# Attention work of a pair moved earlier in the next pair's sums: projection at a pair's end, latents at the next pair's head, key products ahead of the choice

## The reference

```
W = weight * mask[None]                      # weight 16x5000x128, mask 5000x128
h = einsum('bg,egp->bep', x, W) + bias       # 64 x 16 tokens x 128
h = h + attention(layernorm(h))              # causal over the 16 tokens
h = h + ffn(layernorm(h))                    # 64 experts, two per token, and a shared one
```

## Time and profile before

| | us |
|---|---|
| median of 3 runs | 253.7 (252.67 to 255.78) |
| profiled execution | 254.11 |
| its span, first to last instruction | 252.4 |
| PE busy, of 2479 matmuls | 184.7 (73%) |
| DVE busy | 152.0 (60%) |
| POOL busy | 144.1 (57%) |
| ACT busy | 82.4 (33%) |
| mean granted TensorE clock | 0.891 |

### The profile page before, as it was taken

One profiled execution on the slowest core, in us unless ns is written; L12 is line 12 of the kernel. 1 busy time (PEld: TensorE's weight loads), 2 busy tenths in 40 slices (PEclk: granted clock), 3 DMA queues, 4 the chain that ended last, 5 costly groups with the idle time before them and its releaser, 6 DMA issues.

```text
span 252.4 us, 6075 instructions
## 1 busy us (share of the span) xinstructions
PE 184.7 (73%) x2479; PEld 153.9 (61%) x2479; DVE 152.0 (60%) x366; ACT 82.4 (33%) x245; POOL 144.1 (57%) x117
## 2 busy tenths in 40 slices
PE   0057877279989789695896699388976987999810
PEld 0057866169878678584785488257755766678410
DVE  0024382975696888979939928768796249011291
ACT  2004200023343333341331232538664444335500
POOL 3326479259979779999678783103114242074570
PEclk9999999977999999999599599657996599999965
DMA  7999999999999999999999999593011128213432
GB/s 237 256 342 418 361 421 334 403 417 417 417 419 422 417 419 416 426 417 413 396 226 220 227 194 145 153 265 145 4 42 52 55 70 243 87 42 96 139 96 53
DMA packets 32981, 65.11 MB, mean 258 GB/s; under 512 B 2874, under 2 KB 25367, under 8 KB 32375
## 3 DMA queue, kind: packets, MB, share of 16 engines
q1 hardware_dynamic: 31416, 59.47, 71.5%
q10 hardware_dynamic: 576, 3.26, 3.1%
q0 software_dynamic: 960, 1.97, 3.0%
HBM read 56.96 MB, written 7.73 MB: 256 GB/s over the span
## 4 chain that ended last, share of the span: by engine, by line
PE 39%; DVE 19%; DMA 16%; SPq 8%; ACT 7%; issue 4%; POOL 3%; POOLq 1%; DVEq 0%; ACTq 0%
DMA ring<-in_L_tok_weight_dram 15%; PE bank L833 13%; PE bank L1021 4%; SPq L360 4%; PE bank L991 4%; DVE bank L1233 3%; DVE prod L1227 3%; DVE ring L1206 3%; DVE prod L1251 2%; DVE bank L1259 2%; PE bank L1005 2%; SPq L366 2%; PE bank L971 2%; PE bank L876 2%; POOL ring L529 2%
## 5 line engine op out<-in xcount | busy, mean ns | idle before, releaser
L464 POOL TENSOR_TENSOR ring<-ring,mask 128x896 f32<-128x896 f32 (+1 forms) x48 | 91.6, 1933 | 19.0 <-DMA ring<-in_L_tok_weight_dram 19.0
L833 PE MATMUL bank<-ring,xT 128*64 128x128 f32 x1248 | 83.8, 294 | 9.9 <-DVE ring L1206 7.6
L833 PEld LDWEIGHTS bank<-ring,xT 128*64 128x64 f32 x1248 | 76.4, 149 | 14.6 <-DVE ring L1206 9.2
L1206 DVE TENSOR_TENSOR ring<-ring,bank 128x1024 f32<-128x1024 f32 (+1 forms) x45 | 45.7, 1049 | 35.5 <-DMA ring<-in_L_tok_weight_dram 35.5
L453 POOL TENSOR_TENSOR rstd<-mv,half 128x1 f32<-128x1 f32 (+1 forms) x24 | 14.2, 599 | 38.9 <-DVE mv L1214 23.4
L529 POOL DMA_INDIRECT ring<-expert_outputs,slot_index x16 | 16.0, 1002 | 16.9 <-DMA expert_outputs<-ring 8.0
L484 POOL DMA_INDIRECT expert_inputs<-xf,slot_index x14 | 14.3, 1021 | 9.9 <-DVE slot_index L1311 6.9
L814 PE MATMUL bank<-cst,w 64*128 64x64 f32 x39 | 5.3, 328 | 16.1 <-DMA w<-in_x_dram 15.4
L1021 PE MATMUL bank<-w2p,ring 64*64 64x128 f32 (+1 forms) x256 | 14.5, 291 | 3.4 <-ACT ring L705 2.1
L506 POOL TENSOR_TENSOR mask<-ring,mask 128x256 f32<-128x256 f32 x8 | 6.0, 756 | 16.3 <-ACT ring L699 16.3
L991 PE MATMUL bank<-w,ring 128*64 128x128 f32 (+1 forms) x256 | 14.9, 298 | 0.3 <-POOL mask L506 0.3
(11 more groups left out here) (151 smaller groups left out, 302.6 us busy)
## 6 DMA issues: line engine op xcount, KB each, us to landing
ring<-in_L_tok_weight_dram SPq DMA_DIRECT2D x48, 832.0 KB, 13.2
expert_inputs<-w ACTq DMA_DIRECT2D x3, 1024.0 KB, 9.9
ring<-expert_inputs SPq DMA_DIRECT2D x6, 512.0 KB, 5.4
expert_outputs<-ring SPq DMA_DIRECT2D x12, 256.0 KB, 2.3
mask<-in_L_tok_mask_dram SPq DMA_DIRECT2D x3, 832.0 KB, 16.1
w<-in_x_dram SPq DMA_DIRECT2D x1, 1250.0 KB, 13.6
w2p<-in_L_ffn_w_dram SPq DMA_DIRECT2D x1, 1024.0 KB, 18.9
xT<-masks_dram SPq DMA_DIRECT2D x1, 1024.0 KB, 7.9
```

The costliest lines, as they stand in the source:

```text
L464: pool.tensor_tensor(unit(j, q, SPLIT(q // 2), UC), unit(j, q, SPLIT(q // 2), UC), mask[:, (m + SPLIT(q // 2)) * D:(m + UC) * D], ALU.mult ...
L833: last = pe.matmul(bank[0][64 * par:64 * par + 64, 0:D], xT[:, (UC * t + c) * B:(UC * t + c + 1) * B], unit(j, 2 * t + par, c, c + 1), sta ...
L1206: dve.tensor_tensor(both(j, t, a, b), both(j, t, a, b), m.rearrange("p (u f) -> p u f", u=1).to_broadcast([P, 2, (b - a) * D]), ALU.mult). ...
```

## The change

- `project(c-1)` stands at the end of step c, and `turn_xn(c-1)` ahead of its last quarter, in every step from 1 on; so far this was so in step 7 alone, and the others had it at the head of step c+1. `norm_h` and `copy_xnT` move with it on ScalarE, to both sides of `probs`.
- `turn_qk(b)` stands at the head of the step between `turn_o` and `attend`, `qkv(b)` behind quarter 0, `values(b)` behind quarter 1, the gate behind quarter 2, `rank_tokens(d)` behind quarter 3.
- VectorE: `scores` is split; `multiply_keys(b)` and `stats_h(a)` come ahead of `choose(d)`, `sum_scores(b)` behind `place(d)`. Of its pieces one moves each from the third place to the second (`VECTOR_SHARE` 2, 1, 2, 1 to 2, 2, 1, 1).
- GpSimd: one piece, `root_qk`, one piece, `root_h2`, four pieces, in place of three pieces, `root_h2`, `root_qk`, three pieces.
- The order after the steps is as it was.

```
-POOL_SHARE = (3, 3)
-VECTOR_SHARE = (2, 1, 2, 1)
+POOL_SHARE = (1, 1, 4)
+VECTOR_SHARE = (2, 2, 1, 1)
...
                 mask_pieces(POOL_SHARE[0])
-                if d >= 0:
-                    root_h2(d)
                 if b >= 0:
                     root_qk(b)
                 mask_pieces(POOL_SHARE[1])
+                if d >= 0:
+                    root_h2(d)
+                mask_pieces(POOL_SHARE[2])
...
+                if b >= 0:
+                    square_qk(b)
+                    norm_qk(b)
                 if d >= 0:
                     copy_oT(d)
                 if b >= 0:
-                    copy_xnT(b)
-                    square_qk(b)
+                    turned_qk(b)
                 if d >= 0:
                     norm_xf(d)
                 if b >= 0:
-                    norm_qk(b)
+                    heads_k(b)
                 if d >= 0:
                     copy_xfT(d)
                 if b >= 0:
-                    copy_qkv(b)
-                if c == NCH - 1:
+                    heads_v(b)
+                if a >= 0:
                     norm_h(a)
-                    copy_xnT(a)
                 if b >= 0:
                     probs(b)
-                if 0 <= a < NCH - 2:
-                    norm_h(a)
+                if a >= 0:
+                    copy_xnT(a)
...
-                mask_pieces(VECTOR_SHARE[2])
+                if a >= 0:
+                    stats_h(a)
+                if b >= 0:
+                    multiply_keys(b)
                 if d >= 0:
                     choose(d)
-                if a >= 0:
-                    stats_h(a)
+                mask_pieces(VECTOR_SHARE[2])
                 if d >= 0:
                     place(d)
                 if b >= 0:
-                    scores(b)
+                    sum_scores(b)
                     less_max(b)
```

More of the change, by code:

```diff
@@ L606, in copy_xnT @@
                 act.copy(xnT[:], bank[3][:, 0:P]).then_inc(s_xnTs, 1)
-            def copy_qkv(j):
-                turned_qk(j)
-                heads_k(j)
-                heads_v(j)
             def turned_qk(j):
@@ L926, in _ @@
                     pe.wait_ge(s_qw, 16 * 6)
-                    pe.wait_ge(s_centred, 2)
-                project_b, attend_d = b >= 0, d >= 0
+                project_a, qkv_b, attend_d = c >= 1, b >= 0, d >= 0
                 if attend_d:
                     turn_o(d)
-                if project_b:
-                    turn_xn(b)
+                if qkv_b:
+                    turn_qk(b)
                 if attend_d:
                     attend(d)
-                if project_b:
-                    project(b)
-                for n in range(4):
-                    sum_genes(c, n)
+                sum_genes(c, 0)
+                if qkv_b:
+                    qkv(b)
+                sum_genes(c, 1)
                 if attend_d:
                     turn_xf(d)
-                if project_b:
-                    turn_qk(b)
-                sum_genes(c, 4)
+                if qkv_b:
+                    values(b)
+                sum_genes(c, 2)
                 if attend_d:
                     gate(d)
-                if project_b:
-                    qkv(b)
+                sum_genes(c, 3)
                 if attend_d:
                     rank_tokens(d)
-                sum_genes(c, 5)
-                if project_b:
-                    values(b)
-                for n in range(6, 12):
+                for n in range(4, 12):
                     sum_genes(c, n)
-                    if c == NCH - 1 and n == 10:
+                    if project_a and n == 10:
                         turn_xn(c - 1)
-                if c == NCH - 1:
+                if c == 1:
+                    pe.wait_ge(s_centred, 2)
+                if project_a:
                     project(c - 1)
@@ L1217, in over_keys, with multiply_keys @@
                 return q.rearrange("p (a h) d -> p a h d", a=1).to_broadcast([P, n, NH, q.shape[2]])
-            def scores(j):
+            def multiply_keys(j):
                 n, f = 2 * j + 2, NH * DK
@@ L1228, in scores, with sum_scores @@
                 dve.tensor_tensor(pr[:, :, :, DH:DK], keys[:, :, :, DH:DK], over_keys(turned, n), ALU.mult).then_inc(s_prod, 1)
+            def sum_scores(j):
+                n, f = 2 * j + 2, NH * DK
                 dve.wait_ge(s_prod, j + 1)
@@ L1236, in scores @@
                 then(dve.memset(raw(j)[0:64].rearrange("p (h s) -> p h s", h=NH)[:, :, n - 1:n], NEG))
+            def scores(j):
+                multiply_keys(j)
+                sum_scores(j)
             def less_max(j):
```

## The result

The changed kernel takes 265.72 us (median of 4 runs, 264.71 to 275.11) against 253.19 for the kernel before beside it (250.98 to 255.78): ratio 1.0512 [1.0413, 1.0612], **slower by 5%**. I had said 255.4, with a range to 261. The profiled execution spans 262.9 us at a mean clock of 0.867, where before had 252.4 and 0.891. Medians are of all executions, while a ratio and its interval leave out those, like the one of 275.11, in which a kernel ran slower as a whole.

The account below looks back on a forecast made before the run. DMA was taken to pace the early steps, a ring of waits among engines those from 4 on. 254.1 less 2.0 (steps 3 to 7) plus 3.5 (step 2) gave 255.6 for the profiled execution, stated as 255.4, range 250 to 261.

Parts of the forecast that it names:

- I take none in steps 3 to 6 and none in 7: Clock drops at the step heads, 3.0 us each: none counted, 0 to 3 kept open for step 7.
- every head cold: Slower rival: heads of steps 3 to 7 at 1.2 GHz, up to 3.0 us each; two give 261.6, five 270; chance 0.20.
- an idle stretch between 2.3 and 3.5 us: TensorE wait at a head from which the clock was said to drop; the new heads were put at 2 us.
- Step 2, a loss of 3.5: Step 2 ends at 74.2 instead of 70.7 us, 2.5 of it from a low-clock stretch; bounds 1.0 and 4.5.
- The gain of 2.9 in step 6: Step 6 goes from 20.7 to 17.85 us; the 2.0 gain over steps 3 to 7 stands almost wholly there.
- The head of 7.3 us: Handover chain from the projection's end until VectorE can multiply the keys, summed to 7.3 us at full clock.
- `place` at 1.2 us: Term of VectorE's list behind the choice, for placing the tokens' slots: 1.2 us.
- VectorE's way: VectorE's list behind the choice to the step's end: 7.8 us in step 5, 8.6 in step 6.
- CHAIN: Theory set up for the experiments: the new chain of handovers is longer than summed, whatever the clock.
- GpSimd as the bound: Rival: GpSimd's roots and pieces wait, steps run 16.5, 16.5, 19.1; 2 us more, 257.6; shares 0.65 with the forecast.
- VectorE solid: Faster rival: steps come down to VectorE's busy time plus joints, 245.6 us, half of it 250; chance 0.15.
- The remainder's multiply: Multiply of the remainder's weights in step 0, now behind a piece: costed at nothing, else 2 us of DMA backlog.

Follow-up runs that it names:

- hot_rank_bank: hot_step2 with place's ranks and one slot value in a PSUM bank instead of SBUF: 255.12 us, ratio 1.0055 to the kernel before.
- busy_before_fit: Kernel before the change plus 10 and 12 identity products ahead of turn_o in steps 6 and 7: 250.59 us against 252.2, ratio 0.9908.
- hot_step2: Changed kernel plus identity products ahead of turn_qk, 7 in steps 3 to 7, 6 in step 2: 257.36 us; run again 256.88, ratio 1.0161 to before.
- hot_choose_bank: hot_step2 with choose(d) ahead of the key products, plus hot_rank_bank's PSUM edit of place: 254.51 us, ratio 1.0041 to the kernel before.
- project_early_fit: Kernel before with only the projection moved early, plus 3, 7, 12 identity products ahead of turn_o in steps 5, 6, 7: 251.24 us, ratio 0.9922.
- choose_first: Changed kernel with choose(d) ahead of multiply_keys(b) on VectorE again: 271.37 us, ratio 1.067 to the kernel before.
- pool_three: Changed kernel with GpSimd's three pieces ahead of both roots again (POOL_SHARE 3, 0, 3): 282.0 us, ratio 1.1153 to the kernel before.

## Why the prediction was wrong

| | forecast | changed kernel | `hot_rank_bank` |
|---|---|---|---|
| first `turn_o` | 74.2 | 76.4 | 74.3 |
| step 3 | 16.1 | 19.6 | 16.9 |
| step 4 | 16.4 | 17.2 | 16.5 |
| step 5 | 17.25 | 17.9 | 17.1 |
| step 6 | 17.85 | 18.6 | 18.0 |
| step 7 | 17.6 | 20.1 | 17.9 |
| steps 3 to 7 | 85.2 | 93.4 | 86.2 |

The last column is the changed kernel with its clock kept up and `place` freed of GpSimd: the steps 3 to 7 are the forecast's within 1.0 us in all, and step 3 by itself is 0.8 over. From the forecast's 255.6 for an execution like the profiled one to the 264.7 measured are 9.1 us: 2.2 in step 2, 3.5 in step 3, 2.2 in steps 4 to 6, 2.5 in step 7, less 1.3 in the rest. What was wrong is, above all, what I had put at zero.

- **"I take none in steps 3 to 6 and none in 7"** (the clock). This is the failed step. The second rival, "every head cold", was the right mechanism with nearly the right price (3.0 said, 2.8 measured) and had 0.20. Its point of decision, "an idle stretch between 2.3 and 3.5 us", did not hold. Step 3 went cold with 2.56 us, inside that span, while I had put my heads at 2; step 4 stayed warm with 2.05 and step 6 with 0.41 and 1.45; but step 5 went cold for a quarter with 0.59 and 1.29, far below it; step 7 with 1.82 and 1.37 around a single turn, and I had seen that last stretch and set it to nothing, by one row of step 5. One row does not give a threshold, and the length of a single wait does not decide alone.
- **Step 2, a loss of 3.5.** The mechanism was right, the size not: 5.7 us. I took a low stretch of 5 us of work; the window 59.30 to 70.00 shows 10.7 us at clock 0.51 with PE busy 10.3. I had measured it by one row, 52 sums in 4.73 us. At half speed 5 us of busy time cost 2.5 and 10.3 cost 5.1: a difference of 2.6, where the step missed by 2.2. With 6 products ahead of this head the first `turn_o` was at 73.96, where the forecast had 71.7 at the full clock and 74.2 with its low stretch.
- **The gain of 2.9 in step 6** (20.7 to 17.85), on which the whole gain of 2.0 stood. It set a sum at the full clock against a step of before at 0.83. `busy_before_fit` has that step at 18.6 with the old order and the clock at 1.00, and `hot_rank_bank` at 18.0 with the new one. So some 2.1 of the 2.9 were the clock's, and 0.6 the order's.
- **The head of 7.3 us.** In step 5 of `hot_step2`, at the full clock, it is 7.6 from the end of the projection to the key products. Right. At low clock, in step 3, 10.5.
- **`place` at 1.2 us** came from step 5 of before, where they come at the end of GpSimd's pieces: the earlier trace rows has these end at 112.13, and the instruction that adds the ranks took 0.41 us there, to 112.15, a sign that I passed over:

```profile
111.74 0.41 DVE L1308 SCALAR_TENSOR_TENSOR spot<-topi,rank 128x2 f32<-128x2 uint32 x1
```

  In the new order it stands in the middle of four pieces. It took 2.1 in step 5 of `hot_step2`: the mis-sized term, by 0.9, on "VectorE's way", which sets steps 5 and 6. In the changed kernel an instruction of it took 1.54 in step 3 and another 1.56 in step 4. Freeing it took the ratio from 1.0161 to 1.0055. So most of what I had kept for CHAIN was not handovers.
- **GpSimd as the bound**: no, in steps 2 to 6; its roots wait for the squares (2.7 to 7.3 us in steps 2 to 4). In step 7 it held the head, as said: the root ended 1.1 us after `turn_o` began (1.9 in the forecast), and TensorE's gap grew by it.
- **VectorE solid**: no; steps 5 and 6 at the full clock are 1.8 us above its busy time in `hot_step2` and 2.0 to 2.9 in `hot_rank_bank`, by the ring of `o`, head and keys.
- **The remainder's multiply**: right in the end. The sums of pair 1 began at 40.4, 3.7 us later than before and behind a wait of 4.38 us, and ran at clock 0.50 up to 46.0; and yet step 1 ended at 56.3 as forecast.
- **The DMA backlog "hides the later issue"**: it ran dry (194 GB/s in one slice), but neither VectorE nor GpSimd waited for a weight behind 62 us. Right in its effect.
- **The rest shifts**: 93.1 for 94.4 us. Right.

The Trainium skill, TensorE: Matmul & The Clock Gate, section "HAM oscillation — how this bites in real kernels", tells of bursts of some 2 us between DMA waits of some 3 to 5 us, each burst at the low clock again. The prediction read this as "every new head would be cold", which is wider: no single wait at these heads is longer than 2.88 us. Even so the trace has four of the six heads cold (2, 3, 5 and 7; not 4 and 6); I had weighed it and trusted more.

Open: the remaining 0.4 to 0.6% of `hot_rank_bank` and `hot_choose_bank` over before. Their fair partners are kernels of the old order that are kept warm as well, `busy_before_fit` (0.9908) and `project_early_fit` (0.9922), and to these 1.2 to 1.5% are left. The later end of step 2 does not explain it: in `project_early_fit` the first `turn_o` comes at 75.3 and steps 3 to 7 take 82.6 us, against 74.3 and 86.2 in `hot_rank_bank`. The difference lies in step 3 (14.9 against 16.9) and step 7 (15.7 against 17.9), in which the forecast itself had the new order behind, by 0.7 each; it was not taken apart. What would let a head keep its clock without products was not found.

## What to carry to other kernels

Before pulling a chain of short handovers onto the head of a step, ask what TensorE computes meanwhile, and price the chain at both clocks: the half-speed stretch falls on the chain itself. To tell a bad order from a cold clock, put products of the right length in its gap and time it again; too long a filler hides what it should show. Keep both kernels warm before comparing their orders: a loss at low clock can vanish at full clock, and a gain can be the clock's and not the order's. And look for tiny VectorE instructions that end as a GpSimd one ends, before changing how much GpSimd does ahead.

## What the runs showed of the hardware

- A VectorE instruction on 128x2 with both operands in SBUF was held until a GpSimd piece (1.5 to 2.1 us) was over: 1.99 us in place of 0.16 (`choose_first`, step 5), with ends that agree within 0.05 us (129.35 and 129.31 there). It can be held through several pieces that follow one another: 5.20 us over three of them in `pool_three`, step 4. With one operand in PSUM it took 0.17 us under the same kind of pieces in steps 3 to 7 of `hot_rank_bank`. The Trainium skill, SBUF — State Buffer, section "Who interferes with whom", says that a VectorE instruction with two SBUF inputs contends with a GpSimd instruction that reads SBUF, and calls this an exclusive lock. The runs agree.
- A `tensor_scalar` on 128x2 with its one tensor in SBUF was held as well: 1.56 us in step 4 of the changed kernel, 2.13 in step 3 of `pool_three`; from PSUM it took 0.15 (`hot_rank_bank`).
- The granted clock was 0.51 over 10.7 us in which TensorE was busy 10.3 (59.3 to 70.0 us of the changed kernel).
- A product with 64 stationary columns takes as long as one with 128: 14 of them (28 instructions) 3.27 us, 16 (32 instructions) 3.74, so 0.234 each.
